# Attention: query and key products over four graphs, 512 columns at a time

## The chip, the cores and the metric

The kernel runs on one core of one Trainium2 chip. The metric is the device time of one execution in microseconds (us), here the median of three runs.

## The reference

`x` holds 128 graphs of 128 nodes with 512 features, `adj` a 128x128 matrix per graph. The first layer is attention with 16 heads of 32 features, with `2 * adj` as a bias, a residual and a layer norm:

```
q, k, v = x @ Wq.T, x @ Wk.T, x @ Wv.T          # split into 16 heads
a = einsum('bhnd,bhmd->bhnm', q, k) * D**-0.5 + (adj + adj)
p = softmax(a)                                  # rows that are all zero give 0
x = layernorm(x + einsum('bhnm,bhmd->bhnd', p, v) @ Wo.T)
```

The second layer picks one of four experts for each graph, computes `adj @ (x @ W[expert])`, normalises over all graphs of an expert, and adds a residual with a layer norm. Only the attention is touched by the change.

## The kernel before

The attention, the expert layer and the last norm run one after the other. In the attention a step is one graph. Every engine has its own instruction queue, written out in the order of the code, and semaphores order the engines. A loop (`for_steps`) runs 31 times over a body of four steps; the last four steps are written out behind it.

An fp32 product is made of three passes over high and low parts (`passes`), each over four chunks of 128 features, so 12 matmuls accumulate in one PSUM bank. Query and key are computed for several graphs at once: one **unit** (`qk_unit`) is one chunk of 128 output features, and its moving operand is the transposed `x` of `GROUP` graphs, `GN = GROUP * 128` columns. With `GROUP = 2` a unit has 256 columns, a group of two graphs has eight units, and each step issues four of them, for a group that is used later. Banks A and B (4 and 5) take turns; VectorE copies bank A and ScalarE bank B (`copy_qk`).

TensorE's step t, in this order: `transposes(0)` to `transposes(3)` of the normalised probabilities of graph t, each behind a wait on `probs_done`; half of the value product of graph t+2; `weighted_values(0..3)`; `scores` of graph t+1; the other half of the values; unit 0 (`next_unit(0)`); the output product of graph t with Wo, called WO here (line 308); units 1, 2 and 3.

VectorE's step, behind `scores`: 16 minima, `largest`, `inverse` and `scales` for heads 0 to 3, `largest` for heads 4 to 7; then it waits for WO and adds the residual (line 492, `res`); `inverse` and `scales` of heads 4 to 7; `bn_stats`; `copy_qk` of unit 1; `largest`, `inverse`, `scales` of heads 8 to 11; two small norm operations; the same three for heads 12 to 15; `copy_pt` of the next step, `copy_qk` of unit 3, the layer norm's output (line 525, behind GpSimd's `rstd`), and `copy_pt(t, 2)`. GpSimd multiplies each quarter of the probabilities by its scales (`normalise(t+1, c)`, line 553), and with that releases `transposes(c)` of step t+1. So what stands behind `res` on VectorE comes after WO in every step:

```
dve.wait_ge(wo_ps, t + 1)
dve.wait_ge(x_in[s], i * 16 + 16)
nc.vector.tensor_tensor(res[:, s % 2], bank[BANK_WO][:, :], x_nat[:, s], ...
```

Every second step VectorE casts a new group of `x` (`xt_hi`) and GpSimd makes its low part (`xt_low`).

Of the kernel before, what the change touches and what calls it, by code (L numbers as in the profile page):

```python
# [31 lines left out]
GROUP = 2  # L32
# [12 lines left out]
def attention_phase(nc, io, W_hi, W_lo, w_stage, expert_w_in, ident, ones, g_x1, adj_t, hand_over, kept, pair,  # L45
# [5 lines left out]
    GN = GROUP * P  # L51
    UNITS = 2 * C // GROUP
    AHEAD = 12
    Q, K, V, O = range(4)
    e_hi_done, e_lo_done, g_x1_in, g_adj_in, ones_done = hand_over

    with ExitStack() as ctx:
# [11 lines left out]
        xt_stage = kept[:, 24:28].rearrange("p (g a) (b n) -> p g (a b) n", g=2, n=GN)  # L69
        res = kept[:, 28:30]  # L70
        qk = [half[:, :, :].rearrange("p (w a) (b n) -> p w (a b) n", w=2, n=GN) for half in pair]
        xt_hi = sb("xt_hi", [P, 2, C, GN], F32R)
        xt_lo = sb("xt_lo", [P, 2, C, GN], F32R)
        adj_nat = sb("adj_nat", [P, UNROLL, P])
        o_hi = sb("o_hi", [P, C, P], F32R)
        o_lo = sb("o_lo", [P, C, P], F32R)
        neg_max = sb("neg_max", [P, HEADS])
        row_sum = sb("row_sum", [P, HEADS])
        abs_max = sb("abs_max", [P, HEADS])
        inv_sum = sb("inv_sum", [P, HEADS])  # L80
        row_scale = sb("row_scale", [P, HEADS])
# [12 lines left out]
        xt_in = [sem(f"xt_in{i}") for i in range(2)]  # L94
# [15 lines left out]
        minima_begun = sem("minima_begun")  # L110

        LAST = B - UNROLL

        def for_steps(eng, body):

            with eng.Fori(0, LAST // UNROLL) as i:
                for s in range(UNROLL):
                    body(i * UNROLL + s, s, i, False)
            for s in range(UNROLL):
                body(LAST + s, s, LAST // UNROLL, True)  # L120

        def exists(step, last, ahead):
            return not last or step + ahead < B

# [3 lines left out]
        def _(sp):  # L128
            def load_xt(g, p):
                sp.dma_start(xt_stage[:, p], io["x_t"][g]).then_inc(xt_in[p], 16)  # L130

            def load_w(n):
                sp.dma_start(w_stage[:, n % 2], io["w"][n]).then_inc(w_in[n], 16)

            load_xt(0, 0)
            load_w(Q)
            load_w(K)
            load_xt(1, 1)
            sp.dma_start(adj_nat[:, 0], io["adj"][0]).then_inc(adj_in[0], 16)
            for n in (V, O):  # L140
                sp.wait_ge(w_lo_done, n - 1)
                load_w(n)
            for s in range(1, UNROLL):
# [3 lines left out]
            for e in range(2):  # L147

                sp.wait_ge(w_lo_done, V + e + 1)
                sp.dma_start(w_stage[:, e], io["expert_w"][e].rearrange("(c p) k -> p c k", p=P))\  # L150
                  .then_inc(expert_w_in[e], 16)

            def load_expert_w(e, freed):
                sp.wait_ge(e_lo_done, freed)
# [3 lines left out]
            def body(t, s, i, last):  # L158
# [9 lines left out]
                if last and t == B - 1:  # L168
                    load_expert_w(3, 2)
                sp.wait_ge(x1_done, t + 1)  # L170
                sp.dma_start(x1_dram[t], x1[:, s]).then_inc(x1_out[s], 16)
                if last and t == B - 2:
                    load_expert_w(2, 1)
                if last and s == 0:
                    for g in range(UNROLL):
                        sp.wait_ge(x1_out[g], 32)
                        sp.dma_start(g_x1[:, g], x1_dram[g]).then_inc(g_x1_in[g], 16)
                        sp.dma_start(adj_t[:, g, 0:P], io["adj_t"][g]).then_inc(g_adj_in[g], 16)
# [6 lines left out]
        def _(pe):  # L185
            def qk_unit(n, c, which, par, b):

                dst = bank[b][:, 0:GN]
                todo = [(w, x, k) for w, x in passes(W_hi, W_lo, xt_hi, xt_lo) for k in range(C)]
                for m, (w, x, k) in enumerate(todo):  # L190
                    mm = pe.matmul(dst, w[:, which, k, c * P:(c + 1) * P], x[:, par, k, :],  # L191
                                   start=m == 0, stop=m == len(todo) - 1)
                mm.then_inc(qk_ps, 1)

            def v_parts(s, b):

                par, j = (s // 2) % 2, s % 2
# [8 lines left out]
            def scores(s):  # L206

                par, j = (s // 2) % 2, s % 2
                for c in range(C):
                    for r in range(HC):  # L210
                        rows = slice(r * HD, (r + 1) * HD)
                        mm = pe.matmul(bank[r][:, c * P:(c + 1) * P],  # L212
                                       qk[par][rows, Q, c, j * P:(j + 1) * P],
                                       qk[par][rows, K, c, j * P:(j + 1) * P], start=True, stop=True)
# [4 lines left out]
            for n in range(8):  # L219
# [6 lines left out]
                qk_unit(n, n % C, n // C, 0, BANK_B - n % 2)  # L226
            for done in qk_done:
                pe.wait_ge(done, 4)
            scores(0)
            pe.wait_ge(w_lo_done, 3)  # L230
            for s in range(2):
                for _ in v_parts(s, BANK_B - s):
                    pass
            pe.wait_ge(xt_lo_done, 2)
            for n in range(8, AHEAD):
                if n < 10:
                    pe.wait_ge(v_done, n - 7)
                else:
                    pe.wait_ge(qk_done[n % 2], n // 2)
                qk_unit(n, n % C, Q, 1, BANK_B - n % 2)  # L240
            pe.wait_ge(const_done, 3)

            def body(t, s, i, last):
# [24 lines left out]
                if exists(t, last, 2):  # L268
                    pe.wait_ge(res_done, t + 1)
                    values = v_parts((s + 2) % UNROLL, BANK_WO)  # L270
# [10 lines left out]
                if exists(t, last, 1):  # L281


                    for done in qk_done:
                        pe.wait_ge(done, 2 * (t + 1 - (s + 1) % 2) + 4)
                    scores((s + 1) % UNROLL)
                some_values(6)

                def next_unit(k):

                    ahead = s + 3
                    if k == 0 and s % 2:
                        pe.wait_ge(xt_lo_done, i * 2 + ahead // 2 + 1)
                    pe.wait_ge(qk_done[k % 2], AHEAD // 2 + 2 * t + k // 2)
                    qk_unit(AHEAD + 4 * t + k, k, ahead % 2, (ahead // 2) % 2, BANK_B - k % 2)

                more_units = exists(t, last, 3)
                if more_units:
                    next_unit(0)
# [11 lines left out]
                if more_units:  # L311
                    for k in range(1, UNITS):
                        next_unit(k)
# [4 lines left out]
        def _(act):  # L318
            def cut_w(n):
                act.wait_ge(w_in[n], 16)  # L320
                nc.scalar.activation(W_hi[:, n], w_stage[:, n % 2], ACT.Copy).then_inc(w_hi_done, 1)

            def copy_qk(n, c, which, par):
                act.wait_ge(qk_ps, n + 1)
                nc.scalar.activation(qk[par][:, which, c, :], bank[BANK_B][:, 0:GN], ACT.Copy,
# [20 lines left out]
            for n in range(8):  # L346
# [3 lines left out]
                if n % 2 == 0:  # L350
                    copy_qk(n, n % C, n // C, 0)
# [5 lines left out]
            for n in range(8, AHEAD, 2):  # L357
                copy_qk(n, n % C, Q, 1)
            cut_w(O)

            def body(t, s, i, last):
# [7 lines left out]
                ahead = s + 3  # L369
# [4 lines left out]
                for k, heads in ((0, range(3, 9)), (2, range(9, HEADS))):  # L374
                    if exists(t, last, 1):
                        exps(t + 1, heads)
                    if exists(t, last, 3):
                        copy_qk(AHEAD + 4 * t + k, k, ahead % 2, (ahead // 2) % 2)
                if last and t >= B - 3:
                    e = t - (B - 3)  # L380
                    cut_expert(e, *((qk_ps, 4 * B) if e < V else (v_ps, B)))
# [5 lines left out]
        def _(dve):  # L387
            def cut_w(n):
                dve.wait_ge(w_hi_done, n + 1)
                nc.vector.tensor_tensor(W_lo[:, n], w_stage[:, n % 2], W_hi[:, n].bitcast(F32),  # L390
# [7 lines left out]
            def cut_xt(g, p):  # L398
                dve.wait_ge(xt_in[p], 16)
                nc.vector.tensor_copy(xt_hi[:, p], xt_stage[:, p]).then_inc(xt_hi_done, 1)  # L400

            def copy_qk(n, c, which, par):
                dve.wait_ge(qk_ps, n + 1)
                nc.vector.tensor_scalar(qk[par][:, which, c, :], bank[BANK_A][:, 0:GN],
# [36 lines left out]
            dve.sem_inc(res_done, 1)  # L441
            cut_xt(0, 0)
            cut_w(Q)
            cut_w(K)
            cut_xt(1, 1)
            for n in range(8):
                if n == C:
                    cut_w(V)
                if n % 2:
                    copy_qk(n, n % C, n // C, 0)  # L450
# [6 lines left out]
            for n in range(9, AHEAD - 1, 2):  # L457
                copy_qk(n, n % C, Q, 1)
            cut_w(O)
# [6 lines left out]
            copy_qk(AHEAD - 1, C - 1, Q, 1)  # L466

            def body(t, s, i, last):
# [26 lines left out]
                ahead = s + 3  # L495
# [6 lines left out]
                if exists(t, last, 3):  # L502
                    copy_qk(AHEAD + 4 * t + 1, 1, ahead % 2, (ahead // 2) % 2)
# [16 lines left out]
                if exists(t, last, 3):  # L520
                    copy_qk(AHEAD + 4 * t + 3, C - 1, ahead % 2, (ahead // 2) % 2)
# [11 lines left out]
        def _(pool):  # L533
# [10 lines left out]
            def xt_low(g, p):  # L544
                pool.wait_ge(xt_hi_done, g + 1)
                nc.gpsimd.tensor_tensor(xt_lo[:, p], xt_stage[:, p], xt_hi[:, p].bitcast(F32),  # L546
# [8 lines left out]
            xt_low(0, 0)  # L555
            xt_low(1, 1)
# [3 lines left out]
            def body(t, s, i, last):  # L560
                if s % 2 and not last:
# [666 lines left out]
```

## Time and profile before

| | |
|---|---|
| runs | 2770.59, 2771.8, 2773.67 us; median 2771.8 |
| profiled execution | 2769.72 us, span 2768.0 us, granted clock 0.986 |
| TensorE busy | 2662.7 us, 96% of the span |
| VectorE, ScalarE, GpSimd busy | 1918.4, 1514.5, 1282.0 us |
| attention | from the start to about 1992 us |

An engine that is busy for nearly all of a stretch bounds it, unless its instructions only look busy; where it waits, the row says who ended the wait. The granted clock is a share of 2.4 GHz.

### The profile page before, as it was taken

The numbers are of one execution on the slowest core, as the hardware profiler recorded it, in microseconds if no ns is written. First come the engines' busy times: TensorE is split into PE (matmuls) and PEld (weight loads), VectorE is DVE, ScalarE is ACT, GpSimd is POOL, SyncE is SP. The second block draws the span as 40 slices with busy tenths as digits, with TensorE's granted clock in tenths as the row PEclk, the third lists the DMA queues.
The fourth block names the chain that finished last, engine by engine and source line by source line (L and its number), as shares of the span: only waits on it lengthen the run. The fifth ranks groups of instructions, "written<-read, shape, count | busy, mean of one in ns | idle before, by whom it ended". The sixth has DMA issues, their size and how long they took to land. (4 is left out here: it accounts for less than half of the span.)

```text
span 2768.0 us, 77846 instructions
## 1 busy us (share of the span) xinstructions
PE 2662.7 (96%) x22583; PEld 2264.7 (82%) x22584; DVE 1918.4 (69%) x8351; ACT 1514.5 (55%) x5391; POOL 1282.0 (46%) x1174
## 2 busy tenths in 40 slices
PE   8999999999999999999999999999799999997776
PEld 7898989898989888888888888888688888883232
DVE  6777777777777777777777777777733333335887
ACT  5565666666665656565656565656544444442444
POOL 2333334343434333334333433343366666666887
PEclk9999999999999999999999999999899999998998
DMA  4111111111111111111111111111234344445999
GB/s 147 62 53 54 53 62 53 54 53 62 53 54 53 62 54 53 57 58 58 49 58 56 58 49 64 51 57 52 75 123 141 131 138 131 136 134 197 396 405 352
DMA packets 169427, 277.32 MB, mean 100 GB/s; under 512 B 19378, under 2 KB 52146, under 8 KB 168882
## 3 DMA queue, kind: packets, MB, share of 16 engines
q1 hardware_dynamic: 150962, 243.36, 26.2%
q10 hardware_dynamic: 18432, 33.56, 3.2%
q8 instruction: 15, 0.25, 0.0%
q14 instruction: 18, 0.15, 0.0%
HBM read 184.57 MB, written 92.27 MB: 100 GB/s over the span
## 5 line engine op out<-in xcount | busy, mean ns | idle before, releaser
L553 POOL TENSOR_TENSOR kept<-kept,row_scale 128x512 f32<-128x512 f32 x512 | 533.4, 1042 | 1106.5 <-DVE row_scale L437 1096.4
L331 ACT ACTIVATE kept<-kept,neg_max 128x128 f32<-128x128 f32 x2048 | 796.0, 397 | 138.0 <-DVE neg_max L413 138.0
L413 DVE CUSTOM_DVE_ANT_0 kept<-att_bank,adj_nat 128x128 f32<-128x128 f32 x2048 | 442.6, 286 | 3.6 <-PE att_bank L212 1.6
L331 ACT ACTIVATION_READ_ACCUMULATOR kept<-kept,neg_max 128x1 f32 x2048 | 399.9, 195 | 0.0
L422 DVE TENSOR_REDUCE abs_max<-kept 128x4 f32<-128x512 f32 x512 | 349.2, 682 | 0.1
L191 PE MATMUL att_bank<-xt_hi,w_hi 128*128 128x256 f32 x2048 | 329.2, 283 | 11.2 <-DVE w_lo L390 11.2
L191 PE MATMUL att_bank<-xt_hi,w_lo 128*128 128x256 f32 x2048 | 329.7, 283 | 0.0
L191 PE MATMUL att_bank<-xt_lo,w_hi 128*128 128x256 f32 x2048 | 329.1, 283 | 0.0
L191 PEld LDWEIGHTS att_bank<-xt_hi,w_hi 128*128 128x128 f32 x2048 | 298.7, 191 | 30.7 <-issue 10.8
L364 ACT ACTIVATE kept<-att_bank 128x512 f32<-128x512 f32 x256 | 153.2, 599 | 279.8 <-PE att_bank L250 279.6
L191 PEld LDWEIGHTS att_bank<-xt_hi,w_lo 128*128 128x128 f32 x2048 | 282.7, 191 | 0.0
L191 PEld LDWEIGHTS att_bank<-xt_lo,w_hi 128*128 128x128 f32 x2048 | 282.4, 191 | 0.0
L479 DVE TENSOR_TENSOR o_lo<-att_bank,o_hi 128x512 fp32r<-128x512 f32 x128 | 88.5, 692 | 248.7 <-ACT o_hi L367 248.7
L250 PE MATMUL att_bank<-ident,kept 128*128 128x128 f32 x2048 | 248.1, 274 | 6.4 <-POOL kept L553 6.3
L463 DVE COPY kept<-att_bank 128x512 f32<-128x512 f32 x256 | 176.0, 688 | 94.9 <-PE att_bank L250 94.9
L250 PEld LDWEIGHTS att_bank<-ident,kept 128*128 128x128 f32 x2048 | 227.8, 141 | 9.1 <-POOL kept L553 5.4
L546 POOL TENSOR_TENSOR xt_lo<-kept,xt_hi 128x1024 fp32r<-128x1024 f32 x64 | 151.5, 2368 | 126.8 <-DVE xt_hi L475 117.0
L367 ACT ACTIVATE o_hi<-att_bank 128x512 fp32r<-128x512 f32 x128 | 76.5, 597 | 233.8 <-PE att_bank L258 233.8
L989 PE MATMUL ps_z<-n_y,ident 128*128 128x512 f32 x256 | 151.7, 676 | 52.3 <-POOL n_y L1109 47.5
L835 POOL TENSOR_TENSOR out_sum<-out_sum,g_out 128x512 f32 x96 | 123.7, 1289 | 134.9 <-ACT g_out L752 134.9
L1144 ACT ACTIVATE n_x<-n_x,n_nb,n_rstd 128x512 f32<-128x512 f32 x128 | 104.4, 815 | 131.3 <-POOL n_nb L1126 78.9
L752 ACT ACTIVATE g_out<-ps_o 128x512 f32<-128x512 f32 x96 | 57.4, 598 | 217.0 <-PE ps_o L702 217.0
(136 smaller groups left out, 5233.4 us busy)
## 6 DMA issues: line engine op xcount, KB each, us to landing
kept<-in_x_t SPq DMA_DIRECT2D x64, 512.0 KB, 3.5
kept<-in_x SPq DMA_DIRECT2D x128, 256.0 KB, 2.5
x_scratch<-kept SPq DMA_DIRECT2D x128, 256.0 KB, 2.0
g_x<-x_scratch SPq DMA_DIRECT2D x128, 256.0 KB, 2.7
n_x<-x_scratch SPq DMA_DIRECT2D x128, 256.0 KB, 6.2
out_x<-n_x ACTq DMA_DIRECT2D x128, 256.0 KB, 5.4
y_scratch<-g_out SPq DMA_DIRECT2D x96, 256.0 KB, 2.0
n_y<-y_scratch SPq DMA_DIRECT2D x96, 256.0 KB, 5.6
```

The costliest lines, as they stand in the source:

```text
L191: mm = pe.matmul(dst, w[:, which, k, c * P:(c + 1) * P], x[:, par, k, :], start=m == 0, stop=m == len(todo) - 1)
L250: mm = pe.transpose(bank[c][:, r * P:(r + 1) * P], probs[:, h * P:(h + 1) * P], ident[:, :])
L331: nc.scalar.activation(probs[:, h * P:(h + 1) * P], neg_s[:, h * P:(h + 1) * P], ACT.Exp, bias=neg_max[:, h:h + 1], scale=-1.0, accum_out= ...
L364: nc.scalar.activation(probs_t[:, c * D:(c + 1) * D], bank[c][:, :], ACT.Copy).then_inc(pt_odd, 1)
L413: nc.vector.tensor_tensor_reduce(neg_s[:, h * P:(h + 1) * P], bank[r][:, c * P:(c + 1) * P], adj_nat[:, s], -2.0, BIG, ALU.add, ALU.min, n ...
L422: nc.vector.tensor_reduce(abs_max[:, heads], neg_s[:, c * D:(c + 1) * D].rearrange("p (h m) -> p h m", h=HC), AX_X, ALU.max, apply_absolut ...
L463: nc.vector.tensor_copy(probs_t[:, c * D:(c + 1) * D], bank[c][:, :]).then_inc(pt_even, 1)
L546: nc.gpsimd.tensor_tensor(xt_lo[:, p], xt_stage[:, p], xt_hi[:, p].bitcast(F32), ALU.subtract).then_inc(xt_lo_done, 1)
L553: nc.gpsimd.tensor_tensor(part, part, by, ALU.mult).then_inc(probs_done, 1)
L835: nc.gpsimd.tensor_tensor(acc, acc, src, ALU.add).then_inc(sum_done, 1)
L989: pe.matmul(dst, ident[:, :], y[:, s], start=True, stop=False)
L1144: nc.scalar.activation(x1[:, s], x1[:, s], ACT.Identity, bias=nb[:, u, k:k + 1], scale=rstd[:, u, k:k + 1]).then_inc(out_done, 1)
```

## The change

`GROUP` goes from 2 to 4. A unit now has 512 columns, a whole PSUM bank; a group of four graphs has eight units, and a step issues two, one ahead of WO and one behind it. `x` is loaded, cast and cut in one go every fourth step instead of half as much every second step. The loop's body has eight steps and runs 15 times; the last eight steps are written out. Ahead of the loop stand 16 units of 256 columns (group 0 in halves) and two of 512, where 12 of 256 stood. The last eight steps issue 2, 2, 2, 3, 3, 0, 0, 0 units, all of 256 columns. Query and key of every other group lie in `g_x1` and half of `w_stage`; the first two expert matrices are therefore loaded near the end of the attention and not at its start. Small tiles move into unused parts of `kept`.

```diff
-GROUP = 2
+GROUP = 4
-    AHEAD = 12
+    HEAD_UNITS = 4 * C + UNITS
+    TAIL = 2 * UNROLL
+    TAIL_UNITS = [(n, 0) for n in range(UNITS, 2 * C)] + [(n, 1) for n in range(UNITS, 2 * C)]
+    TAIL_COUNTS = (2, 2, 2, 3, 3, 0, 0, 0)
...
-        LAST = B - UNROLL
+        LAST = B - TAIL
...
-            with eng.Fori(0, LAST // UNROLL) as i:
-                for s in range(UNROLL):
-                    body(i * UNROLL + s, s, i, False)
+            with eng.Fori(0, LAST // TAIL) as i:
+                for s in range(TAIL):
+                    body(i * TAIL + s, s % UNROLL, i * 2 + s // UNROLL, s // UNROLL, False)
...
-                if s % 2 == 0 and not last:
-                    g = i * 2 + s // 2
-                    sp.wait_ge(xt_lo_done, g + 1)
-                    load_xt(g + 2, s // 2)
+                if s == 0 and not last:
+                    sp.wait_ge(xt_lo_done, i * 2 + 4)
+                    load_xt(i + 2)
...
+                units = units_of_step(t, s, g, last)
+                for k, unit in enumerate(units[:1]):
+                    next_unit(*unit, place_of(t, k, last))
...
-                if more_units:
-                    for k in range(1, UNITS):
-                        next_unit(k)
+                for k, unit in enumerate(units[1:], 1):
+                    next_unit(*unit, place_of(t, k, last))
...
-                if exists(t, last, 3):
-                    copy_qk(AHEAD + 4 * t + 1, 1, ahead % 2, (ahead // 2) % 2)
+                for unit, k in here:
+                    if k == 0:
+                        copy_qk(*unit)
...
-                if s % 2 and not last:
+                if s == 2 and not last:
 
-                    dve.wait_ge(v_ps, t + 1)
-                    dve.wait_ge(xt_in[s // 2], i * 16 + 32)
-                    nc.vector.tensor_copy(xt_hi[:, s // 2], xt_stage[:, s // 2]).then_inc(xt_hi_done, 1)
+                    dve.wait_ge(v_ps, t + 2)
+                    dve.sem_inc(xt_turn, 1)
+                    dve.wait_ge(xt_in, i * 16 + 32)
+                    for half in range(2):
+                        cut_xt(g, half)
```

TensorE in a step of the loop, from the last value matmuls on. Before, with a unit in three rows of line 191 and WO in three of line 308 (two more units follow):

```order
L200 MATMUL att_bank<-w_hi,xt_lo 128x512 x4
L294 REGISTER_ALU
L191 MATMUL att_bank<-xt_hi,w_hi 128x256 x4
L191 MATMUL att_bank<-xt_lo,w_hi 128x256 x4
L191 MATMUL att_bank<-xt_hi,w_lo 128x256 x4
L303 REGISTER_ALU
L308 MATMUL att_bank<-w_hi,o_hi 128x512 x4
L308 MATMUL att_bank<-w_lo,o_hi 128x512 x4
L308 MATMUL att_bank<-w_hi,o_lo 128x512 x4
L191 MATMUL att_bank<-xt_hi,w_hi 128x256 x4
L191 MATMUL att_bank<-xt_lo,w_hi 128x256 x4
L191 MATMUL att_bank<-xt_hi,w_lo 128x256 x4
```

The same place in the changed kernel, where a unit is line 224 and WO line 345, and the transposes follow:

```order
L232 MATMUL att_bank<-w_hi,xt_lo 128x512 x4
L224 MATMUL att_bank<-xt_hi,w_hi 128x512 x4
L224 MATMUL att_bank<-xt_lo,w_hi 128x512 x4
L224 MATMUL att_bank<-xt_hi,w_lo 128x512 x4
L340 REGISTER_ALU
L345 MATMUL att_bank<-w_hi,o_hi 128x512 x4
L345 MATMUL att_bank<-w_lo,o_hi 128x512 x4
L345 MATMUL att_bank<-w_hi,o_lo 128x512 x4
L224 MATMUL att_bank<-xt_hi,w_hi 128x512 x4
L224 MATMUL att_bank<-xt_lo,w_hi 128x512 x4
L224 MATMUL att_bank<-xt_hi,w_lo 128x512 x4
```

Of 1024 unit columns in a step, 256 stood ahead of WO and 768 behind it; now 512 stand on either side.

VectorE in a step, from `res` on. Before, with `copy_qk` of unit 1 in line 404:

```order
L492 TENSOR_TENSOR kept<-att_bank,kept 128x512
L430 RECIPROCAL inv_sum<-row_sum 128x4
L435 REGISTER_ALU
L437 SCALAR_TENSOR_TENSOR row_scale<-abs_max,inv_sum 128x4
L501 BN_STATS stats<-kept 128x6
L403 REGISTER_ALU
L404 TENSOR_SCALAR out_sum<-att_bank 128x256
L420 REGISTER_ALU
L422 TENSOR_REDUCE abs_max<-kept 128x4
```

The changed kernel in the same place:

```order
L541 TENSOR_TENSOR kept<-att_bank,kept 128x512
L471 RECIPROCAL kept<-kept 128x4
L476 REGISTER_ALU
L478 SCALAR_TENSOR_TENSOR kept<-kept 128x4
L550 BN_STATS stats<-kept 128x6
L461 REGISTER_ALU
L463 TENSOR_REDUCE kept<-kept 128x4
```

One copy has left the stretch between `res` and the last scales; nothing else behind `res` moved.

## Rows read from the trace of the kernel before

**Rows 1.** Busy time in one stretch: PE, PEld, DVE, ACT, POOL, PEclk, DMA share, GB/s.
```profile
800.00:1200.00 400.00, 400.00 (x3964) 358.25 (x3963) 308.55 (x1421) 241.24 (x997) 152.88 (x144) 1.00 0.17 55
```
**Rows 2.** TensorE's timeline over one step: start, duration, operation, count.
```profile
1004.00 1.91 PE L250 MATMUL att_bank<-ident,kept 128*128 128x128 f32 x16
1005.67 1.17 PE L200 MATMUL att_bank<-w_hi,xt_hi 128*128 128x512 f32 x4
...
1010.83 0.65 PE L191 MATMUL att_bank<-xt_hi,w_hi 128*128 128x256 f32 x4
1012.27 1.10 PE L308 MATMUL att_bank<-w_hi,o_hi 128*128 128x512 f32 x4
...
1015.02 0.64 PE L191 MATMUL att_bank<-xt_hi,w_hi 128*128 128x256 f32 x4
...
1019.33 1.91 PE L250 MATMUL att_bank<-ident,kept 128*128 128x128 f32 x16
```
**Rows 3.** TensorE's timeline, WO of another step.
```profile
1917.48 1.07 PE L308 MATMUL att_bank<-w_lo,o_hi 128*128 128x512 f32 x4
...
1919.29 0.64 PE L191 MATMUL att_bank<-xt_hi,w_hi 128*128 128x256 f32 x4
```
**Rows 4.** VectorE's timeline from the residual on, same step.
```profile
1015.22 0.69 DVE L492 TENSOR_TENSOR kept<-att_bank,kept 128x512 f32<-128x512 f32 x1 [0.51 <-PE att_bank L308]
...
1016.11 0.69 DVE L501 BATCH_NORM_STATS2 stats<-kept 128x6 f32<-128x512 f32 x1
1016.71 0.41 DVE L404 TENSOR_SCALAR out_sq<-att_bank 128x256 f32<-128x256 f32 x1
1017.03 0.68 DVE L422 TENSOR_REDUCE abs_max<-kept 128x4 f32<-128x512 f32 x1
...
1019.02 0.16 DVE L437 SCALAR_TENSOR_TENSOR row_scale<-abs_max,inv_sum 128x4 f32<-128x4 f32 x1
```
**Rows 5.** GpSimd's and ScalarE's timelines, same step: last scaling, last exponential.
```profile
1019.26 1.04 POOL L553 TENSOR_TENSOR kept<-kept,row_scale 128x512 f32<-128x512 f32 x1
...
1016.62 0.40 ACT L331 ACTIVATE kept<-kept,neg_max 128x128 f32<-128x128 f32 x1
```
**Rows 6.** Timeline of all engines, step 125, which has no units.
```profile
1964.07 1.08 PE L308 MATMUL att_bank<-w_hi,o_lo 128*128 128x512 f32 x4
...
1965.19 0.69 DVE L492 TENSOR_TENSOR kept<-att_bank,kept 128x512 f32<-128x512 f32 x1 [0.33 <-PE att_bank L308]
...
1966.08 0.68 DVE L501 BATCH_NORM_STATS2 stats<-kept 128x6 f32<-128x512 f32 x1
...
1966.80 0.69 DVE L422 TENSOR_REDUCE abs_max<-kept 128x4 f32<-128x512 f32 x1
...
1967.85 2.19 POOL L553 TENSOR_TENSOR kept<-kept,row_scale 128x512 f32<-128x512 f32 x2 [0.56 <-DVE row_scale L437]
...
1968.76 0.16 DVE L437 SCALAR_TENSOR_TENSOR row_scale<-abs_max,inv_sum 128x4 f32<-128x4 f32 x1
...
1970.10 1.12 PE L250 MATMUL att_bank<-ident,kept 128*128 128x128 f32 x4 [0.50 <-POOL kept L553]
```
**Rows 7.** VectorE and GpSimd timelines: idle ahead of `o_lo` and of scaling.
```profile
1024.33 0.69 DVE L479 TENSOR_TENSOR o_lo<-att_bank,o_hi 128x512 fp32r<-128x512 f32 x1 [2.29 <-ACT o_hi L367]
...
1014.16 1.04 POOL L553 TENSOR_TENSOR kept<-kept,row_scale 128x512 f32<-128x512 f32 x1 [4.40 <-DVE row_scale L437]
```
**Rows 8.** TensorE's timeline, step 0.
```profile
41.15 0.65 PE L258 MATMUL att_bank<-kept 128*32 128x128 f32 x16 [0.63 <-DVE kept L463]
```
**Rows 9.** The page's DMA: a code queue (packets, MB), an issue (KB, us to land).
```profile
q8 instruction: 15, 0.25, 0.0%
...
adj_nat<-in_adj SPq DMA_DIRECT2D x128, 64.0 KB, 2.8
```
**Rows 10.** Busy time at the attention's end, columns as in rows 1.
```profile
1960.00:1970.00 10.00, 6.19 (x30) 4.11 (x28) 8.99 (x49) 9.05 (x35) 4.12 (x5) 1.00 0.26 82
1970.00:1980.00 10.00, 7.21 (x80) 5.36 (x80) 9.34 (x41) 6.29 (x29) 1.55 (x3) 0.83 0.08 28
```

More of the change, by code:

```diff
@@ L50, in attention_phase, with columns, units_so_far, units_of_step @@
     HALF_SCALE = 0.5 * float(D) ** -0.5
-    GN = GROUP * P
+    GN, HALF_N = GROUP * P, GROUP * P // 2
     UNITS = 2 * C // GROUP
-    AHEAD = 12
+    HEAD_UNITS = 4 * C + UNITS
+    TAIL = 2 * UNROLL
     Q, K, V, O = range(4)
+    def columns(half):
+        return slice(0, GN) if half is None else slice(half * HALF_N, (half + 1) * HALF_N)
+    TAIL_UNITS = [(n, 0) for n in range(UNITS, 2 * C)] + [(n, 1) for n in range(UNITS, 2 * C)]
+    TAIL_COUNTS = (2, 2, 2, 3, 3, 0, 0, 0)
+    def units_so_far(t):
+        if t < B - TAIL:
+            return HEAD_UNITS + UNITS * t
+        return HEAD_UNITS + UNITS * (B - TAIL) + sum(TAIL_COUNTS[:t - (B - TAIL)])
+    def units_of_step(t, s, g, last):
+        if not last:
+            first = (s + 1) % UNROLL * UNITS
+            par = (g + 1 + (s + 1) // UNROLL) % 2
+            return [(HEAD_UNITS + UNITS * t + k, first + k, None, par) for k in range(UNITS)]
+        m = units_so_far(t) - units_so_far(B - TAIL)
+        return [(units_so_far(B - TAIL) + m + k, *TAIL_UNITS[m + k], 1)
+                for k in range(TAIL_COUNTS[t - (B - TAIL)])]
     e_hi_done, e_lo_done, g_x1_in, g_adj_in, ones_done = hand_over
@@ L93, in attention_phase @@
         w_hi_done, w_lo_done = sem("w_hi_done"), sem("w_lo_done")
-        xt_in = [sem(f"xt_in{i}") for i in range(2)]
+        xt_first, xt_in = [sem(f"xt_first{i}") for i in range(2)], sem("xt_in")
         x_in = [sem(f"x_in{i}") for i in range(UNROLL)]
@@ L356, in _, with body @@
             exps(0, range(12, HEADS))
[L357 to L361, printed above, removed]
+            for n in range(2 * C, 4 * C, 2):
+                copy_qk(n, n - 2 * C, 1, 0)
+                if n == 3 * C - 2:
+                    cut_w(O)
+            copy_qk(4 * C, 0, None, 1)
+            def body(t, s, i, g, last):
                 for c in (1, 3):
@@ L368, in body @@
                                      ACT.Copy).then_inc(o_hi_done, 1)
-                ahead = s + 3
+                here = [(unit, k) for k, unit in enumerate(units_of_step(t, s, g, last)) if place_of(t, k, last) == 0]
                 if exists(t, last, 1):
@@ L449, in _ @@
                 if n % 2:
-                    copy_qk(n, n % C, n // C, 0)
+                    copy_qk(n, n, 0, 0)
+            dve.wait_ge(xt_in, 16)
+            for half in range(2):
+                cut_xt(1, half)
             dve.wait_ge(s_ps, 1)
@@ L456, in _ @@
                 scales(0, c)
-            for n in range(9, AHEAD - 1, 2):
-                copy_qk(n, n % C, Q, 1)
-            cut_w(O)
+            for n in range(2 * C + 1, 4 * C, 2):
+                copy_qk(n, n - 2 * C, 1, 0)
+                if n == 3 * C - 1:
+                    cut_w(O)
             def copy_pt(t, c):
@@ L493, in body @@
                                         ALU.add).then_inc(res_done, 1)
-                ahead = s + 3
+                here = [(unit, k) for k, unit in enumerate(units_of_step(t, s, g, last)) if place_of(t, k, last) == 1]
                 if more:
@@ L501, in body @@
                 nc.vector.bn_stats(stats[:, s % 2], res[:, s % 2]).then_inc(stats_done, 1)
-                if exists(t, last, 3):
-                    copy_qk(AHEAD + 4 * t + 1, 1, ahead % 2, (ahead // 2) % 2)
+                for unit, k in here:
+                    if k == 0:
+                        copy_qk(*unit)
                 dve.wait_ge(stats_done, t + 1)
@@ L519, in body @@
                     copy_pt(t + 1, 0)
-                if exists(t, last, 3):
-                    copy_qk(AHEAD + 4 * t + 3, C - 1, ahead % 2, (ahead // 2) % 2)
+                for unit, k in here:
+                    if k > 0:
+                        copy_qk(*unit)
                 dve.wait_ge(rstd_done, t + 1)
@@ L553, in normalise, with body @@
                 nc.gpsimd.tensor_tensor(part, part, by, ALU.mult).then_inc(probs_done, 1)
-            xt_low(0, 0)
-            xt_low(1, 1)
+            for n in range(4):
+                xt_low(n + 1, n // 2, n % 2)
             for c in range(C):
                 normalise(0, c)
-            def body(t, s, i, last):
-                if s % 2 and not last:
-                    xt_low(i * 2 + s // 2 + 2, s // 2)
+            def body(t, s, i, g, last):
+                if s == 2 and not last:
+                    for half in range(2):
+                        xt_low(i * 2 + 5 + half, g, half)
                 if exists(t, last, 1):
```

183 lines of the change are left out of this document (100 added, 83 removed).

## The prediction, made blind

> **What bounds the kernel now.** I read the busy time by stretches first, then TensorE's timeline over one step, then the timelines of the engines that release it. In the attention's steady state TensorE is busy for 400.0 of 400 us at full clock [rows 1]. One step takes 1019.33 - 1004.00 = 15.33 us, and no row of TensorE in it has idle time [rows 2]. So the reader sees a stage whose time is the spacing of its matmuls, and anything that makes them denser should pay. That holds only while every wait of TensorE is over before it is reached, so I next ask how early they are over. The tightest is the wait ahead of the fourth group of transposes, for GpSimd's scaling of heads 12 to 15. That scaling ends at 1019.26 + 1.04 = 1020.30 [rows 5]. The 16 transposes take 1005.67 - 1004.00 = 1.67 us [rows 2], so the fourth group starts three quarters in: at 1019.33 + 1.25 = 1020.58. The cover is 0.28 us.
>
> What sets the scaling's end? Going back: it starts 0.24 us behind VectorE's last scales, and these end a chain that runs without a gap from the residual `res` at 1015.22 [rows 4]. In front of `res` VectorE sat idle for 0.51 us, and TensorE's WO ended that. ScalarE isn't the limit: its last exponential starts at 1016.62 [rows 5], well ahead of the last scales at 1019.02. So there is a second cycle beside TensorE's own work: WO, `res`, the scales, GpSimd, the fourth transposes, and then TensorE's work up to the next WO. It is 0.28 us short of deciding.
>
> **The change part by part.** I call E the moment when TensorE has issued WO.
>
> *Denser matmuls.* Three units of 256 columns take 1019.33 - 1015.02 = 4.31 us, so one takes 1.437 and each of its 12 matmuls 119.7 ns. Eight matmuls of 512 columns take 1919.29 - 1917.48 = 1.81 us [rows 3], 226.3 ns each, so a unit of 512 takes 2.715. Each pair of small units that becomes a large one saves 2.874 - 2.715 = 0.159 us. There are 242 large units (2 ahead of the loop, 2 in each of 120 steps): 38.4 us less work for TensorE. A step of the loop would be 15.33 - 0.32 = 15.01 us of work.
> The Trainium skill (TensorE: Matmul & The Clock Gate, "Wait — 56ns, not 53.3ns?") puts the fixed cost of a warm matmul at about 2.5 ns. By that the 2904 matmuls saved would give 7 us, and unit 0 would take 2.84 us in place of 2.715; with the cycle below the time would be about 2891 us. The rows show about 13 ns each, and I go by the rows.
>
> *The place of WO.* The unit ahead of WO grows from 1.437 to 2.715 us, so E moves back by 1.28 us within the step, while the work behind E shrinks from three small units (4.31) to one large (2.72). From E, TensorE reaches the fourth transposes 2.72 + 1.25 = 3.97 us later. Is the scaling ready by then? Step 125 of the kernel before shows that chain by itself: it has no units, VectorE has no `copy_qk` there, as in the new order, and TensorE waits. WO's last group starts at 1964.07 and takes 0.91 us to issue, so E is 1964.98; `res` starts at 1965.19, `bn_stats` at 1966.08, the next reduction at 1966.80 (0.72 us behind it, where the step with the copy has 1017.03 - 1016.11 = 0.92), the last scales at 1968.76, GpSimd's pair ends at 1967.85 + 2.19 = 1970.04, and the fourth transposes start at 1970.10 [rows 6]. That is 5.12 us from E. The step in the loop gives the same by sum: 0.20 to `res`, 5.08 to the end of the scaling, less 0.20 for the copy, 0.06 to wake, 5.14. So TensorE waits 5.12 - 3.97 = 1.15 us in each step, partly ahead of the third group, the rest ahead of the fourth.
>
> The new period is that of this cycle. From the fourth transposes to unit 0: 1010.83 - 1005.25 = 5.58 us. Unit 0 and WO: 2 x 2.715 = 5.43. From E to the fourth transposes: 5.12. Sum 16.13 us, against 15.33: +0.80 us. It runs 120 times (units of steps 0 to 119): **+96 us**.
>
> The wait moves nothing else onto the path. Queued behind the waiting transposes are the rest of the step; `copy_pt(t, 2)` on VectorE stands behind the `rstd` that GpSimd makes after the same scaling, as before, and TensorE needs it as long after the fourth transposes as before.
>
> *Casts.* VectorE's two casts in one step out of four take about 1.2 us together; they lie in the 2.29 us that VectorE waits ahead of `o_lo` in a step without a cast [rows 7]. GpSimd's low part doubles in that step; one more of it fits in the 4.40 us that it waits ahead of its first scaling even behind the first low part. Without that cover each would cost what it overlaps, once in four steps. `copy_qk` on VectorE falls from two small copies to one large, behind the last scales. The loads of `x` are twice the size and half as many, two steps ahead of their use. ScalarE's copy of unit 0 is ready 1.28 us later, but stands behind six exponentials that end at about the same moment. All at nothing, bounds 0 to +0.1 us a step.
>
> *Ahead of the loop.* Four more small units and two large: 5.75 + 5.43 = 11.2 us. Cutting Wo moves ahead of the loop's first step, where it held a copy and cost TensorE 0.63 us [rows 8]. **+10.6 us**. The first `x` of group 1 could come late and hold the first minima; I take 0, bound +3.
>
> *The last eight steps.* In steps 120 to 124 a small unit stands ahead of WO again: 5.58 + 1.44 + 2.75 + 5.12 = 14.89 us each, now all bound by the chain, against 15.33. Five times -0.44, and 0.2 back where VectorE's copy returns in step 124: **-2 us**. Steps 125 to 127 don't change.
>
> Sum: 96 + 10.6 - 2 = +104.6. The profiled execution took 2769.7 us (its span and 1.7 us around it), so 2874.3; the median of the runs lies 2.1 us above it: **2876 us**.
>
> **The rivals.**
> 1. *The chain isn't longer than its cover, and the denser matmuls come through: faster.* Then TensorE stays fully busy and the time is 2771.8 - 38.4 - 0.6 = 2733 us. For it speaks that TensorE never idles now. Against it: E to the fourth transposes would have to take at most 3.97 us, and rows of two different steps give 5.12 and 5.14. The point from which the time falls at all is 15.33 - 11.01 - 0.07 = 4.25 us (0.07 for the other terms spread over 120 steps). Chance 0.04, with 0.02 more for something between that ends within 0.2%.
> 2. *Code must be loaded again.* TensorE's body of eight steps is nearly twice as long as the one of four. Before, one queue that loads code moved 15 packets in all, over 31 passes of the loop [rows 9]: the bodies stayed where they were. If the longer ones don't, each of 15 passes waits at its start. No row prices such a wait; the nearest is a load of 64 KB, which lands after 2.8 us [rows 9], and 1.15 us of that would fall into the wait that is there anyway. So it is between 0 and 1.65 us a pass: up to +25, 2901 us. I take nothing, since the queue was quiet. Chance 0.10.
> The Trainium skill (Runtime: NRT & Kernel Launch, "Instruction fetch mechanics") says that a taken branch whose target isn't held must fetch its page first, and gives TensorE room for 2048 instructions. No row here shows it.
> 3. *The clock falls.* TensorE would be busy for 15.01 of 16.13 us, 93%. At the attention's end ten microseconds with 62% busy still ran at the full 2.4 GHz, and the next ten fell towards 1.2 GHz [rows 10]. If waits of 2.4 us in a step (14.89 less 12.5 of work) were enough to lower it in steps 120 to 124, the 9.77 us of matmuls between the fourth transposes and E could take up to twice as long, five times: +49, 2925 us. Chance 0.04.
>
> **How the numbers follow.** The forecast has 0.80. Its own range: the chain is 5.12 +- 0.1 us, 12 us over 120 steps; 0 to +3 ahead of the loop; 0 to +6 for covered work that shows in one step of four: 2862 to 2897. The second rival reaches a little above it, so 2858 to 2902 holds more than 8 in 10. Faster 0.04, same 0.02, slower 0.94; 0.2% (5.5 us) is about what this measurement tells from no change.
>
> **What would show it.** In the changed profile: steps 16.1 us apart; TensorE idle about 1.1 us a step ahead of the transposes, ended by GpSimd's scaling; VectorE idle about 1.8 us ahead of `res`, ended by WO; matmuls of a unit 226 ns apart; about 93% busy. Wrong would be the prediction if VectorE did less between `res` and the last scales than the rows show, or if the transposes followed the unit without a gap.

## The result and the profile after

The changed kernel takes 2944.18 us (median of four runs, 2942.12 to 2946.7) against 2771.49 us before: a ratio of 1.0622, 95% interval 1.061 to 1.0635. It is slower by 173 us, and the forecast was 2876 us with a range up to 2902. The direction and the main mechanism came out; two sizes, and a rival that was taken at nothing, did not. (Two of ten executions of the kernel before, in the batch of experiments 5 to 8, fell into a slow state at 5223 and 3331 us and stand in no ratio here.)

Busy time of the same stretch as [rows 1], in the same columns:

```profile
800.00:1200.00 400.00, 376.76 (x3062) 297.50 (x3063) 283.30 (x1279) 216.83 (x888) 141.72 (x132) 1.00 0.16 53
```

TensorE is no longer full: it is busy for 94% of the stretch. Its granted clock is at the full 2.4 GHz but for one fall, shown below. Its timeline over one step of the changed kernel, for [rows 2]:

```profile
1003.93 0.66 PE L286 MATMUL att_bank<-ident,kept 128*128 128x128 f32 x4 [0.54 <-POOL kept L605]
...
1009.53 1.09 PE L224 MATMUL att_bank<-xt_hi,w_hi 128*128 128x512 f32 x4
1010.45 1.10 PE L224 MATMUL att_bank<-xt_lo,w_hi 128*128 128x512 f32 x4
1011.38 1.09 PE L224 MATMUL att_bank<-xt_hi,w_lo 128*128 128x512 f32 x4
1012.32 1.09 PE L345 MATMUL att_bank<-w_hi,o_hi 128*128 128x512 f32 x4
...
1015.11 1.09 PE L224 MATMUL att_bank<-xt_hi,w_hi 128*128 128x512 f32 x4
...
1017.91 1.03 PE L286 MATMUL att_bank<-ident,kept 128*128 128x128 f32 x8
1019.15 0.66 PE L286 MATMUL att_bank<-ident,kept 128*128 128x128 f32 x4 [0.21 <-POOL kept L605]
1020.35 0.66 PE L286 MATMUL att_bank<-ident,kept 128*128 128x128 f32 x4 [0.54 <-POOL kept L605]
```

The fourth group of transposes starts at 1003.93 and again at 1020.35 (and 1036.76): a step is 16.41 us. It waits for GpSimd, and so does the third. The cycle of the prediction is there, piece by piece: 5.60 us to unit 0, 5.58 for unit 0 and WO, then 1020.35 - 1015.11 = 5.24 us from E to the fourth transposes. The unit behind E takes 2.80 us of that and twelve transposes 1.25, so TensorE loses 1.19 us a step there; the waits in brackets say less, since they count from the modelled end of a matmul. VectorE and GpSimd in that last stretch, for [rows 4] and [rows 5]:

```profile
1015.31 0.69 DVE L541 TENSOR_TENSOR kept<-att_bank,kept 128x512 f32<-128x512 f32 x1 [1.98 <-PE att_bank L345]
...
1016.20 0.69 DVE L550 BATCH_NORM_STATS2 stats<-kept 128x6 f32<-128x512 f32 x1
1017.01 0.69 DVE L463 TENSOR_REDUCE kept<-kept 128x4 f32<-128x512 f32 x1
...
1019.01 0.16 DVE L478 SCALAR_TENSOR_TENSOR kept<-kept 128x4 f32<-128x4 f32 x1
...
1019.25 1.04 POOL L605 TENSOR_TENSOR kept<-kept 128x512 f32<-128x512 f32 x1 [0.15 <-DVE kept L478]
```

VectorE now sits idle for 1.98 us ahead of `res` until WO ends; it was 0.51 [rows 4]. Three things aren't in the forecast. Four matmuls of 512 columns start 0.93 us apart and not 0.905 [rows 3], 233 ns each. And once in eight steps, where the loop branches back, VectorE stands still for 2.46 us with nothing to wait for, and TensorE then waits for it:

```profile
1122.43 0.69 DVE L510 COPY kept<-att_bank 128x512 f32<-128x512 f32 x1 [2.46 <-issue]
...
1123.17 0.65 PE L294 MATMUL att_bank<-kept 128*32 128x128 f32 x16 [1.62 <-DVE kept L510]
```

And behind one of these branches, which cost 3.6 us in place of about 1.9, TensorE's granted clock was at the lower of its two levels, 1.2 GHz. The stretch, in the columns of [rows 1]:

```profile
989.30:992.50 3.20, 3.20 (x33) 2.59 (x28) 2.21 (x16) 1.47 (x7) 0.00 (x0) 0.50 0.36 141
```

The queues that load code moved 15 and 18 packets before; now (same view as [rows 9]):

```profile
q8 instruction: 163, 2.67, 0.4%
q14 instruction: 194, 1.59, 0.2%
```

TensorE's waits of the whole changed kernel, by who ended them: us in total, times, longest.

```profile
PE att_bank L286 <- POOL kept L605: 103.4, 252, 2.9
...
PE att_bank L294 <- DVE kept L510: 23.1, 14, 1.9
```

Where the 174.3 us of span lie, with the start of the fourth transposes as the mark. Ahead of step 0: 52.26 against 38.53, +13.7. Steps 0 to 119: 1999.8 against 1840.4, +159.4; of this 120 x (16.41 - 15.33) = 130, and 30 are the 14 branches, 13 of them at 1.9 to 2.2 us and the one with the lower clock at 3.6. Steps 120 to 124: 74.8 against 76.6, -1.8. The rest: +3.0.

### The profile page after: what moved, and what is told of

It is laid out like the page before. It is cut to its first block and busy times, and to the rows that moved or that the text cites. A ratio compares the mean times of both kernels' runs of the same rounds, so it can differ in the third digit from the quotient of the medians.

```text
span 2942.3 us, 70674 instructions
## 1 busy us (share of the span) xinstructions
PE 2710.6 (92%) x19679; PEld 2102.4 (71%) x19680; DVE 1924.3 (65%) x8230; ACT 1491.5 (51%) x5270; POOL 1295.0 (44%) x1174
## 5 line engine op out<-in xcount | busy, mean ns | idle before, releaser
L605 POOL TENSOR_TENSOR kept<-kept 128x512 f32<-128x512 f32 x512 | 532.5, 1040 | 1318.1 <-DVE kept L478 1315.4
L368 ACT ACTIVATE kept<-kept 128x128 f32<-128x128 f32 x2048 | 793.5, 392 | 138.5 <-DVE kept L454 138.5
L454 DVE CUSTOM_DVE_ANT_0 kept<-att_bank,kept 128x128 f32<-128x128 f32 x2048 | 442.7, 286 | 3.4 <-PE att_bank L243 1.8
L368 ACT ACTIVATION_READ_ACCUMULATOR kept<-kept 128x1 f32 x2048 | 391.1, 191 | 0.0
L463 DVE TENSOR_REDUCE kept<-kept 128x4 f32<-128x512 f32 x512 | 350.6, 685 | 14.9
L224 PE MATMUL att_bank<-xt_hi,w_hi 128*128 128x512 f32 (+1 forms) x1080 | 282.7, 383 | 13.9 <-DVE w_lo L430 13.3
L224 PE MATMUL att_bank<-xt_hi,w_lo 128*128 128x512 f32 (+1 forms) x1080 | 284.0, 384 | 0.0
L224 PE MATMUL att_bank<-xt_lo,w_hi 128*128 128x512 f32 (+1 forms) x1080 | 283.7, 384 | 0.0
L224 PEld LDWEIGHTS att_bank<-xt_hi,w_hi 128*128 128x128 f32 x1080 | 198.6, 189 | 57.1 <-issue 13.0
L598 POOL TENSOR_TENSOR xt_lo<-kept,xt_hi 128x1024 fp32r<-128x1024 f32 x64 | 163.3, 2568 | 76.6 <-DVE xt_hi L440 76.6
L232 PE MATMUL att_bank<-w_lo,xt_hi 128*128 128x512 f32 x512 | 173.9, 421 | 0.0
```

The lines of the kernel that those rows point to most:

```text
L232: mm = pe.matmul(bank[b][:, :], x[:, par, k, j * P:(j + 1) * P], w[:, V, k, :], start=m == 0, stop=m == len(todo) - 1)
L368: nc.scalar.activation(probs[:, h * P:(h + 1) * P], neg_s[:, h * P:(h + 1) * P], ACT.Exp, bias=neg_max[:, h:h + 1], scale=-1.0, accum_out= ...
L454: nc.vector.tensor_tensor_reduce(neg_s[:, h * P:(h + 1) * P], bank[r][:, c * P:(c + 1) * P], adj_nat[:, s], -2.0, BIG, ALU.add, ALU.min, n ...
L463: nc.vector.tensor_reduce(abs_max[:, heads], neg_s[:, c * D:(c + 1) * D].rearrange("p (h m) -> p h m", h=HC), AX_X, ALU.max, apply_absolut ...
L598: nc.gpsimd.tensor_tensor(xt_lo[:, par, :, at], xt_stage[:, :, at], xt_hi[:, par, :, at].bitcast(F32), ALU.subtract).then_inc(xt_lo_done, 1)
L605: nc.gpsimd.tensor_tensor(part, part, by, ALU.mult).then_inc(probs_done, 1)
```

## Experiments

Experiments 1 to 4, 6 and 7 were each executed once, beside the kernel before at 2773 us (2769 to 2774 in the second batch). So differences of a few us between them mean nothing by themselves; the steps read in their traces carry the argument.

**1. The kernel before, two units ahead of WO.** Nothing has 512 columns here but what had it before; only the place of WO moves.

```diff
                 if more_units:
                     next_unit(0)
+                    next_unit(1)
...
-                    for k in range(1, UNITS):
+                    for k in range(2, UNITS):
```

> The kernel before, with its units of 256 columns, but two of them ahead of the output product (WO) and two behind. Theory (the place of WO in the step sets the time): the chain from WO over the residual, the scales and GpSimd to the fourth transposes takes 5.34 us here (VectorE's copy of unit 1 is still in it), so a step takes 5.58 + 2.87 + 2.75 + 5.34 = 16.54 us in place of 15.33, and the kernel 2771 + 125 x 1.21 = 2922 us. Rival (the 512 columns themselves or the loop cost the time): no change, 2771 us.

Measured: 2924.71 us. TensorE's timeline:

```profile
1000.67 0.66 PE L250 MATMUL att_bank<-ident,kept 128*128 128x128 f32 x4 [0.17 <-POOL kept L554]
...
1006.25 0.64 PE L191 MATMUL att_bank<-xt_hi,w_hi 128*128 128x256 f32 x4
...
1011.87 0.64 PE L191 MATMUL att_bank<-xt_hi,w_hi 128*128 128x256 f32 x4
...
1014.02 0.74 PE L191 MATMUL att_bank<-xt_hi,w_hi 128*128 128x256 f32 x4 [0.56 <-DVE out_sum L405]
...
1017.20 0.66 PE L250 MATMUL att_bank<-ident,kept 128*128 128x128 f32 x4 [0.17 <-POOL kept L554]
```

A step is 16.53 us, against 16.54 from the sum, and the pieces agree too: 5.58 us to the first unit, 5.62 for two units and WO, 5.33 from E (1011.87) to the fourth transposes. This kernel keeps the short loop, the groups of two and the operands' places. Moving one unit of 1.44 us in front of WO costs 152 us by itself, so the cycle through WO is what bounds, whatever the width of a matmul. The row at 1014.02 shows a second face of the same lateness, bank A's copy, which stands behind `res` on VectorE.

**2. The changed kernel, loop written out.** `for i in range(LAST // TAIL)` in place of `with eng.Fori(0, LAST // TAIL) as i`; the order on each engine is the same.

> The changed kernel with the attention's loop written out, no branch in it. Theory (each pass of the long loop body loads code again, and VectorE stands still for about 2 us for it): the gap of about 1.95 us every eighth step is gone, 15 times, 2944 - 29 = 2915 us, other steps unchanged at 16.41 us. Rival (the gap has another cause, such as the transfer of x that is issued in the same step): 2944 us and the gap stays.

Measured: 2896.68 us, 47.5 less, where 29 were expected. The gap is gone. So is something else: a step takes 16.28 us and not 16.41. VectorE's timeline shows where most of it went:

```profile
1007.67 0.69 DVE L541 TENSOR_TENSOR kept<-att_bank,kept 128x512 f32<-128x512 f32 x1 [2.02 <-PE att_bank L345]
...
1008.56 0.69 DVE L550 BATCH_NORM_STATS2 stats<-kept 128x6 f32<-128x512 f32 x1
1009.28 0.69 DVE L463 TENSOR_REDUCE kept<-kept 128x4 f32<-128x512 f32 x1
...
1011.25 0.16 DVE L478 SCALAR_TENSOR_TENSOR kept<-kept 128x4 f32<-128x4 f32 x1
```

From `bn_stats` to the next reduction it is 0.72 us here and 0.81 in the loop. In the loop, the order shows a register instruction there, which computes the value of a wait; written out, the value is a constant. That this instruction is the cause follows from the order and isn't shown by itself; it stands at 0.09 of the 0.14 us by which the chain is shorter. The fourth transposes come 5.10 us behind E (1012.58 - 1007.48), the 5.12 of [rows 6], which were read in a step that is written out too. 120 x 0.13 = 16 us and 31 us of branches make the 47. The code queues still moved 136 and 118 packets here, and in the loop's steps neither TensorE nor VectorE shows a stop for them: what costs is the branch back, not the loading.

**3. The changed kernel, operands at equal offsets.** The tile `adj_t` shrank in the change from 160 to 136 columns in four rows, 2560 to 2176 bytes, that is from 5 x 512 to 4.25 x 512; so transposed `x` and `o`, allocated behind it, moved against the weights, which are ahead of it, by 384 bytes. The edit allocates it ahead of the weights.

```diff
+            adj_t = cut.enter_context(nc.sbuf_tensor("adj_t", [P, UNROLL, P + 8], F32))
             W_hi = cut.enter_context(nc.sbuf_tensor("w_hi", [P, 4, C, D], F32R))
             W_lo = cut.enter_context(nc.sbuf_tensor("w_lo", [P, 4, C, D], F32R))
             g_x1 = cut.enter_context(nc.sbuf_tensor("g_x1", [P, UNROLL, D], F32))
-            adj_t = cut.enter_context(nc.sbuf_tensor("adj_t", [P, UNROLL, P + 8], F32))
```

> The changed kernel with adj_t allocated ahead of the weights in SBUF, so that weights, transposed x and o start at the same offset within 512 bytes, as in the kernel before; nothing else. Theory (matmuls of 512 columns are 233 and not 226 ns apart because the stationary and the moving operand lie at different offsets): 226 to 227 ns again, a step 0.16 to 0.24 us shorter, 2944 - 19 to 29 = 2915 to 2925 us. Rival (they are slower because units and WO of 512 columns follow each other, or through the surroundings): 233 ns and 2944 us.

Measured: 2928.2 us, 16 less. TensorE's timeline, units and WO:

```profile
1001.52 1.07 PE L224 MATMUL att_bank<-xt_lo,w_hi 128*128 128x512 f32 x4
1002.43 1.07 PE L224 MATMUL att_bank<-xt_hi,w_lo 128*128 128x512 f32 x4
1003.33 1.07 PE L345 MATMUL att_bank<-w_hi,o_hi 128*128 128x512 f32 x4
1004.24 1.07 PE L345 MATMUL att_bank<-w_lo,o_hi 128*128 128x512 f32 x4
1005.15 1.07 PE L345 MATMUL att_bank<-w_hi,o_lo 128*128 128x512 f32 x4
```

Four start 0.905 us apart again, and a step takes 16.27 us. The rival (wide matmuls that follow each other are slower) falls: here they follow each other too. The step gave 17 us; four branches with a lower clock, where the changed kernel has one, took 5 back, and the ends of the kernel gave the rest.

**4. The changed kernel, first unit split around WO.** Six of its 12 matmuls stand ahead of WO, six behind; the sum stays open in bank B meanwhile.

```diff
-                for k, unit in enumerate(units[:1]):
-                    next_unit(*unit, place_of(t, k, last))
+                first = next_unit(*units[0], place_of(t, 0, last)) if units else iter(())
+                for _ in range(12 if last else SPLIT):
+                    next(first, None)
...
+                for _ in first:
+                    pass
...
-                        if late == (k > 0):
+                        if late == (k > 0 or not last):
```

> The changed kernel with only six of the 12 matmuls of the first unit ahead of WO, the other six behind it, and ScalarE's copy of that unit behind its last exponential. Theory (place of WO): WO ends 1.4 us earlier in the step, its chain of 5.24 us is covered by 18 matmuls of 233 ns and 1.25 us of transposes (5.45 us), the waits for GpSimd are gone but for the one at the loop's branch, steps of 15.2 to 15.3 us, 2944 - 120 x 1.15 = 2806 us. Rival (GpSimd or VectorE are the limit for another reason, such as the doubled casts): waits stay and the time is above 2900 us.

Measured: 2794.13 us, 150 less, where 138 were expected. Steps are 15.23 us, and no transposes wait; of TensorE's waits in the attention's loop only the branch is left:

```profile
PE att_bank L300 <- DVE kept L520: 19.0, 14, 1.5
```

The doubled casts and low parts, which run here as in the changed kernel, cost nothing.

**5. The kernel before, one tile narrower.** `[P, UNROLL, P + P // 4]` becomes `[P, UNROLL, P + 8]`.

> The kernel before with one number changed: adj_t has 136 and not 160 columns, so the transposed x and o move by 128 bytes against the weights, as in the changed kernel. Theory (offsets of the operands within 512 bytes): the 24 matmuls of 512 columns of a step take 233 and not 226 ns each, 0.16 us a step, 2771 + 20 = 2791 us, perhaps a few us of change in the expert layer. Rival: no change, 2771 us.

Measured: 2780.27 us, ratio 1.0032 (1.002 to 1.0044): slower by 8 and not by 20. WO's groups start 0.93 us apart:

```profile
1002.40 1.09 PE L308 MATMUL att_bank<-w_hi,o_hi 128*128 128x512 f32 x4
1003.34 1.10 PE L308 MATMUL att_bank<-w_lo,o_hi 128*128 128x512 f32 x4
1004.27 1.09 PE L308 MATMUL att_bank<-w_hi,o_lo 128*128 128x512 f32 x4
1005.20 0.64 PE L191 MATMUL att_bank<-xt_hi,w_hi 128*128 128x256 f32 x4
```

A step is 15.40 us against 15.33. Of the matmuls of 512 columns only those of WO became slower, and of these only its second and third group: 8 in a step, where the expectation counted 24. The first group took as long in the kernel before: WO took 2.75 us there [rows 2], and the second and third group 1.81 of it [rows 3]. The ones of the values already took 0.92 us for four inside a step before, and the ones of 256 columns take 0.48 for four in both.

**6. The kernel before, eight steps in the loop's body.** Order and instructions as before, half as many branches.

```diff
-            with eng.Fori(0, LAST // UNROLL) as i:
-                for s in range(UNROLL):
-                    body(i * UNROLL + s, s, i, False)
+            with eng.Fori(0, LAST // (2 * UNROLL)) as i:
+                for s in range(2 * UNROLL):
+                    body(i * (2 * UNROLL) + s, s % UNROLL, i * 2 + s // UNROLL, False)
+            for s in range(UNROLL):
+                body(LAST - UNROLL + s, s, LAST // UNROLL - 1, False)
```

> The kernel before with eight steps in the loop's body and 15 passes (four steps more written out behind it); every instruction and its order are the same. Theory (code is loaded again in each pass once VectorE's or TensorE's body doesn't fit): the queues that load code move over 100 packets, TensorE waits about 1.5 to 2 us once in eight steps, 2771 + 15 x 1.5 to 2 = 2794 to 2801 us. Rival (the long body is covered): 2771 us.

Measured: 2822.3 us, +50, more than expected: 50 / 14 = 3.6 us a branch.

```profile
1027.83 1.91 PE L252 MATMUL att_bank<-ident,kept 128*128 128x128 f32 x16
...
1045.23 3.61 PE L252 MATMUL att_bank<-ident,kept 128*128 128x128 f32 x16 [1.91 <-issue]
...
1062.29 1.91 PE L252 MATMUL att_bank<-ident,kept 128*128 128x128 f32 x16
```

Busy time and clock while these transposes run, in the columns of [rows 1]:

```profile
1045.40:1048.70 3.30, 3.30 (x17) 3.30 (x17) 1.48 (x3) 0.60 (x1) 0.00 (x0) 0.50 0.04 11
```

TensorE itself stops for 1.91 us behind the branch, its next 16 transposes take twice as long because the granted clock is 1.2 GHz, and two steps take 34.46 in place of 30.66 us. So two costs stand in this branch. Behind 7 of the 14 branches the clock fell like this, each time after a stop of 1.9 to 2.2 us, and they cost 3.8 to 4.0 us; the other seven had stops of 1.8 to 2.2 us at the full clock, and a second one of 0.6 to 1.1 us a little later, and cost 2.9 to 3.6. What decides between them stays open. The code queues moved 193 and 195 packets. A pass of the body holds about 575 to 590 instructions of VectorE here and in the changed kernel, and 2540 and 2140 of TensorE; the body of four steps has 300 and 1270. Half as many branches cost 50 us more: it is the body's length, not the branch alone, that decides whether code is loaded again.

**7. The changed kernel with halves.** Each unit of the loop is again two of 256 columns, one ahead of WO and three behind.

```diff
-            return [(HEAD_UNITS + UNITS * t + k, first + k, None, par) for k in range(UNITS)]
+            return [(HEAD_UNITS + STEP_UNITS * t + k, first + k // 2, k % 2, par) for k in range(STEP_UNITS)]
...
-                    if k == 0:
+                    if k == 0 or k == 1 and not last:
                         copy_qk(*unit)
```

> The changed kernel with every unit of the loop again in two halves of 256 columns, one half ahead of WO and three behind it: groups of four graphs, body of eight steps, loads and casts stay as changed, the 512 columns and the place of WO are undone. Theory (sum of the parts): step 15.33 + 0.16 for the slower 512-column matmuls of values and WO = 15.49, 1.95 us at each of 15 branches, about 8 us ahead of and behind the loop: 2771 + 20 + 29 + 8 = 2828 us. Rival (groups of four, their casts in one step and GpSimd's doubled low part cost the time): above 2900 us.

Measured: 2835.61 us; steps of 15.40 us. That is also the step of experiment 5, so the groups of four graphs, with their loads and casts, add nothing to it. That the total came near the 2828 expected is partly luck: the step is 0.09 us shorter than its term (11 us in all), while the 14 branches took 44 us more than in the kernel before, where 29 were expected.

**8. The three repairs together** (2, 3 and 4), as measured against the kernel before.

> The changed kernel with the three repairs together: the loop written out, operands at equal offsets, six matmuls of the first unit ahead of WO. Theory: TensorE is the limit again, with 48 matmuls of 512 columns at 226 ns a step: 15.21 - 0.32 + small = 14.9 to 15.05 us in place of 16.41, and no gap at branches: 2944 - 120 x 1.4 - 29 - 3 = 2744 us, faster than before by 1%. Rival (each repair uncovers a further wait): between 2771 and 2810 us.

Measured: 2744.77 us, ratio 0.9903 (0.9885 to 0.9921): faster than the kernel before by 1.0%. Steps are 15.02 us, and TensorE is full again:

```profile
800.00:1200.00 400.00, 400.00 (x3432) 330.70 (x3431) 313.34 (x1424) 238.92 (x975) 160.02 (x147) 1.00 0.19 59
```

**9. Offsets in the expert layer.** Two small tiles are allocated behind the expert layer's `y_hi` and `y_lo`, so that these start at the weights' offset; in the kernel before, and in that of experiment 8.

```diff
-        router_w = sb("router_w", [P, C, E])
-        router_b = sb("router_b", [1, E])
         y_hi, y_lo = sb("y_hi", [P, UNROLL, D], F32R), sb("y_lo", [P, UNROLL, D], F32R)
+        router_w = sb("router_w", [P, C, E])
+        router_b = sb("router_b", [1, E])
```

> The kernel before, with the two router tiles of the expert layer allocated behind y_hi and y_lo and not ahead of them, so that y (stationary) and the weights (moving) start at the same offset within 512 bytes; nothing else. Theory (equal offsets make a matmul of 512 columns some 7 ns shorter, wherever it stands): four expert matmuls start 0.905 and not 0.94 us apart, 1536 of them, 2772 - 10 = 2762 us. Rival (the effect belongs to the attention's surroundings): 2772 us.

> The kernel of the three repairs with the same change in the expert layer. Theory: 2745 - 10 = 2735 us, about 1.3% faster than the kernel before. Rival: 2745 us.

Measured: 2766.71 us, ratio 0.9983 (0.9974 to 0.9993), half of what was expected; and 2743.03 us, ratio 0.99 (0.9883 to 0.9916), which can't be told from experiment 8. Four matmuls of a product that stand directly behind others of it, the last four and half of the middle fours, now take 0.91 us and not 0.94; the first four, and those behind another kind of matmul, changed by only 0.01 (1.02 to 1.03 before, 1.01 to 1.02 now).

## Why the prediction was wrong

**The cycle through WO** was right as a mechanism. The wait stood where it was put, experiment 1 met its sum to 0.01 us a step, and its pieces, with no unit wider than before, and experiment 4 took 150 us away by moving six matmuls. That the wait came out nearly as forecast, 1.19 us against 1.15, is partly luck: the chain is 0.12 us longer than assumed, and the unit that covers it is 0.08 us longer too. The period has only the chain in it, and grows by the whole 0.12.

**"That is 5.12 us from E"** was mis-sized: the loop has 5.24. The row came from a step that is written out; between `bn_stats` and the reduction, where the loop has a register instruction, it shows 0.72 us and the changed kernel 0.81. The cross-check by sum (5.14) took the copy's price, 0.20, from the same place, and so repeated the error; experiment 1, with the copy in the chain, has 5.33, so taking the copy out gave only 0.09. 120 x 0.12 = 14 us.

**"Unit 0 and WO: 2 x 2.715 = 5.43"** was mis-sized: 5.58. The spacing of 226 ns was read right, but it belongs to a placement that the change undid through a tile that the prediction doesn't mention, `adj_t`. 120 x 0.15 = 18 us; in experiment 3 unit 0 and WO take 5.46 us, and the step is shorter by 0.14.

**"Code must be loaded again ... I take nothing"** failed. This is the largest single miss. The rival with 0.10 is what happened, and its price a branch was 1.9 to 2.2 us where the bound said 1.65, and 3.6 once, where the clock was lower: about 30 us in the loop. Experiment 2 takes it away with the branches, experiment 6 brings it into the kernel before with nothing but a longer body. It shows on VectorE, which the rival didn't look at; its bound took only TensorE's wait as cover.

The rest held: casts, low parts and loads at nothing (experiments 4 and 7), the last eight steps at -2 (-1.8), and the clock, but for the fall at one branch. The head cost 13.7 and not 10.6 us: the first matmul started at 13.35 us, against 11.18, because the first load of the weights had landed 2.2 us later; two more such loads were under way by then, which before were issued only at 11.06 us. The profiled executions lie 174.3 us apart where 104.6 were forecast. Of the 70 us between, 14 are the chain, 18 unit 0 and WO, 30 the branches, 3 the head, 3 what lies behind step 124, whose cause stays open, and the rest hundredths of a us in each step; the medians miss by 68. No single step explains why the range was missed: even its upper end without the rival, 2897, with the rival's full 25 us on top is 2922 us. All the misses lay on the same side.

The denser matmuls were real, but only those ahead of E stood on the path, and there the unit of 512 columns is longer than the one of 256 that it replaced. What they are worth, with all else repaired, is experiment 8's step of 15.02 us against 15.33.

## What to carry to other kernels

A wide unit is also a long one: before widening, find the instruction in the middle of the step that starts the longest chain on the other engines, and keep what stands ahead of it short, if need be by splitting an accumulation around it. Read a chain's length from a step of the same kind as the one that will run, in the loop or written out, since the two differ by about 0.1 us here. After a change, check two things that are easily passed over in a diff: whether a longer loop body still stays on the engine (the packets of the code queues), and where tiles came to lie. And where a matmul takes twice its time, read the granted clock of that stretch before looking for another cause.

## What was not expected of the hardware

- Matmuls of 512 columns in a row are 226 ns apart when stationary and moving operand start at the same offset within 512 bytes, and 233 ns when they are 128 or 384 bytes apart from that, as experiments 3 and 5 show in either direction. Experiment 3 moves the weights and leaves transposed `x` and `o` in place, experiment 5 the reverse, so it is not the place of one of them alone. What in the chip makes the difference, and which offsets are good in general, stays open; the value products (231 ns on average in the last group of a step, in all kernels) and the groups directly behind another kind of matmul hardly followed the rule.
- The fp32r matmuls of 256 columns hardly changed with the offset: 119.9 to 120.2 ns on average from start to start in the kernel before, 119.9 to 120.7 in experiment 5.
- With a body of eight steps the code queues moved 163 to 195 packets, with one of four 15 and 18. At the full clock a branch cost 1.6 to 2.2 us where VectorE's stop decided, and 2.8 to 3.6 us where TensorE's did (experiments 6 and 7).
- TensorE's granted clock fell to 1.2 GHz behind some of these stops, which lasted 1.6 to 2.2 us: once in 14 branches in the changed kernel, 4 times in experiment 3, 7 times in experiment 6, twice in experiment 7 and never in experiment 4. Nowhere else between step 0 and step 120 did it fall, not in the steps of the changed kernel either, where TensorE waits for 1.19 us in each.
- The chain of 5.24 us on VectorE and GpSimd was 0.14 us shorter with the loop written out; 0.09 of it lies where the loop has a register instruction for the value of a wait.
